# Per-item adapters gathered by GpSimd instead of selected by TensorE, with new chunk counts and a moved style network

## What is computed

```python
hidden = gelu(einsum('bsd,ad->bsa', x, down_W) + down_b)
idx = clip(domain_id, 0, E - 1)
expert_out = einsum('bsa,boa->bso', hidden, expert_W[idx]) + expert_b[idx][:, None, :]
domain_output = where(valid, expert_out, hidden)
hidden = einsum('bsa,da->bsd', domain_output + domain_emb[idx], up_W) + up_b
x = layer_norm(hidden + x) * ln_gamma + ln_beta
...
h = layer_norm(x) * ln_g + ln_b
h_norm = (h - h.mean(1)) * rsqrt(h.var(1) + 1e-08)      # over an item's 64 tokens
sty = relu(hyp(subj_emb[subject_ids]) @ sty_w1 + sty_b1) @ sty_w2 + sty_b2
h = h_norm * softplus(gamma) + beta
gates, idx = top_k(softmax(h @ router_w), 2)
y = sum over the two experts of gate * (relu(h @ w1 + b1) @ w2 + b2)
return x + y
```

## Time and profile before

| | us |
|---|---|
| median of 3 executions | 582.35 (581.31 to 584.63) |
| profiled execution, device time | 582.23 |
| profiled execution, span | 580.3 |
| busy: TensorE, VectorE, ScalarE, GpSimd | 529.5, 379.2, 277.4, 244.4 |
| indirect DMA instructions on GpSimd | 64 scatters (L574), 71 adding stores (L605) |

### The profile page before, as it was taken

One profiled execution on the slowest core, in us unless ns is written; L12 is line 12 of the kernel. 1 busy time (PEld: TensorE's weight loads), 2 busy tenths in 40 slices (PEclk: granted clock), 3 DMA queues, 4 the chain that ended last, 5 costly groups with the idle time before them and its releaser, 6 DMA issues.

```text
span 580.3 us, 15539 instructions
## 1 busy us (share of the span) xinstructions
PE 529.5 (91%) x4386; PEld 445.6 (77%) x4387; DVE 379.2 (65%) x1233; ACT 277.4 (48%) x628; POOL 244.4 (42%) x208
## 2 busy tenths in 40 slices
PE   4977878888776999999999999999999999999993
PEld 3765656566455988988888888888888888888772
DVE  2466989888989868668765464554645655554552
ACT  3547776677563664344253442533424434343432
POOL 2000458888866724766242232322423324223322
PEclk8669797788797999999999999999999999999998
DMA  9465355775454343446644234342342433424222
GB/s 246 152 207 183 110 155 172 254 229 192 165 181 113 83 62 41 102 85 136 133 74 65 38 50 59 40 69 37 46 64 37 62 47 45 55 29 57 39 27 29
DMA packets 78094, 57.58 MB, mean 99 GB/s; under 512 B 51346, under 2 KB 71699, under 8 KB 77907
## 3 DMA queue, kind: packets, MB, share of 16 engines
q1 hardware_dynamic: 63698, 38.37, 25.7%
q0 software_dynamic: 13296, 17.83, 18.0%
q10 hardware_dynamic: 1058, 0.85, 0.7%
HBM read 23.18 MB, written 24.55 MB: 82 GB/s over the span
## 4 chain that ended last, share of the span: by engine, by line
PE 70%; POOL 13%; DVE 6%; issue 4%; DMA 3%; ACT 2%; SPq 1%; POOLq 0%; DVEq 0%; ACTq 0%
PE banks L830 33%; PE banks L846 30%; POOL queues L574 8%; POOL rsT L582 3%; POOL rs L565 2%; PE banks L653 2%; DMA out<-nb,token 1%; DVE w_low L1250 1%; DVE stats L1167 1%; PE banks L713 1%; DMA uw<-up_b 1%; PE banks L693 1%; PE banks L714 1%; DMA rT<-queues 1%; PE banks L727 1%
## 5 line engine op out<-in xcount | busy, mean ns | idle before, releaser
L605 POOL DMA_INDIRECT out<-nb,token x71 | 114.9, 1618 | 221.0 <-ACT nb L1041 196.9
L830 PE MATMUL banks<-rT,w_high 128*128 128x256 f16 (+1 forms) x1248 | 196.7, 265 | 8.4 <-DMA rT<-queues 7.6
L846 PE MATMUL banks<-w_high,stage 128*128 x1136 | 188.1, 273 | 0.9 <-issue 0.2
L830 PE MATMUL banks<-rT,w_low 128*128 128x256 f16 (+1 forms) x624 | 163.3, 264 | 0.0
L846 PE MATMUL banks<-w_low,stage 128*128 x568 | 154.8, 273 | 0.0
L1025 ACT ACTIVATE xb<-banks,feat 128x256 f32<-128x256 f32 (+1 forms) x312 | 120.8, 454 | 52.6 <-PE banks L830 46.3
L830 PEld LDWEIGHTS banks<-rT,w_high 128*128 x1248 | 114.5, 98 | 27.3 <-issue 10.4
L846 PEld LDWEIGHTS banks<-w_high,stage 128*128 128x128 f16 x1136 | 110.4, 98 | 14.8 <-issue 1.9
L1041 ACT ACTIVATE nb<-act,gate 128x256 f32<-128x256 f32 x71 | 32.6, 501 | 179.2 <-DVE act L1508 175.7
L1483 DVE TENSOR_TENSOR stage<-xb,stage 128x512 f16<-128x512 f32 (+1 forms) x156 | 100.6, 645 | 5.3
L1481 DVE CAST stage<-xb 128x512 f16<-128x512 f32 (+1 forms) x156 | 66.6, 427 | 54.3 <-ACT xb L1025 51.6
(11 more groups left out here) (186 smaller groups left out, 516.7 us busy)
## 6 DMA issues: line engine op xcount, KB each, us to landing
stage<-expert_w SPq DMA_DIRECT2D x32, 512.0 KB, 4.6
xb<-x SPq DMA_DIRECT2D x8, 512.0 KB, 6.3
out<-rb SPq DMA_DIRECT2D x8, 512.0 KB, 3.2
queues<-pad_row SPq DMA_DIRECT2D x9, 260.0 KB
out<-nb,token POOLq DMA_INDIRECT x71, 3.9
queues<-h_rows,slot POOLq DMA_INDIRECT x64
b<-exp_b SPq DMA_DIRECT2D x1, 1024.0 KB, 6.5
rT<-queues SPq DMA_TRANSPOSE x39, 4.0
```

What stands on the lines that cost most here:

```text
L605: nc.gpsimd.indirect_dma_start(out=out, out_offset=bass.IndirectOffsetOnAxis(ap=token[:, i.par, s:s + 1], axis=0), in_=yg[:, i.par, s, :], ...
L830: last = nc.tensor.matmul(ps_in(i, c), w[:, at], features(i)[:, v, k, :], start=(n == 0), stop=(n == 3 * DC - 1))
L846: last = nc.tensor.matmul(ps_out(i.par)[:, s, :], v[:, i.par, c, s * P:(s + 1) * P], w[:, at], start=(n == 0), stop=(n == 3 * FC - 1))
```

## The change

GpSimd fetches the adapters itself. VectorE computes row numbers (id x 64 + row), and GpSimd issues 32 indirect loads (`gather`), each of 128 rows of 64 numbers: two items' adapters below each other, 4 loads a group. Those of groups 0 to 3 stand before its loop, those of 4 and 5 at the end of pass 1, those of 6 and 7 at the end of pass 2. TensorE turns them with 4 transposes a group (`turn_rows`), group g+1 in pass g behind up; ScalarE copies them to `wsel` (`copy_adapters`). The table, `select` and its copies are gone. TensorE runs down(0) first, then the item rows, 18 products that nobody reads (`FIRST_WARM`), and group 0's transposes.

Passes have 6, 4, 4, 4, 3, 3, 3, 3 chunks and 2 remain. SyncE loads the next x ahead of the chunks, and a pass's fourth chunk behind the store of x1. The second x waits for group 0's gathers. The ids go out first on ScalarE's queue; the style network's and the norms' constants go out on SyncE's. `style_layer` 2 stands behind down(1), 3 behind the adapters, `style_out` behind up(1); `softplus` stands between `layer_norm` and `scale_features` of group 0 with a table load for Gelu behind it, and `item_gammas` moves to pass 2.

```diff
@@ -54,16 +54,21 @@
-CUTS = [8, 3, 3, 3, 3, 3, 3, 3, 3]
+CUTS = [6, 4, 4, 4, 3, 3, 3, 3, 2]
...
+ROWS_AT = CHUNKS - GROUPS // 2
+ADAPTERS_AT = ROWS_AT - GROUPS
+PAIR = 2 * A
+GATHERS = GROUP // T // 2
...
+FIRST_WARM = 18
@@ -226,9 +233,9 @@
-        table = w_low[0:NONE_ROW + 1, 16 * CHUNK:24 * CHUNK].bitcast(F32)
-        wsel = w_low[0:A, 24 * CHUNK:32 * CHUNK].bitcast(F32)
...
+        wrows = w_low[:, ROWS_AT * CHUNK:CHUNKS * CHUNK].bitcast(F32)
+        wsel = w_low[0:A, ADAPTERS_AT * CHUNK:ROWS_AT * CHUNK].bitcast(F32)
+        table_rows = adapter_w.rearrange("n (o a) -> (n o) a", a=A)
@@ -451,12 +457,15 @@
-                sp.dma_start(ids_i, spread(ids, SUBJECTS)).then_inc(ids_loaded, 16)
-                sp.dma_start(sids_i, spread(subject_ids, SUBJECTS)).then_inc(ids_loaded, 16)
...
+                for dst, src in ((dw[:], down_w), (ab[:, 0:1], down_b)):
+                    sp.dma_start(dst, src).then_inc(down_loaded, 16)
+                for dst, src in ((uw[0:A], up_w), (uw[A:A + 1], up_b)):
...
+                for dst, src in ((g0[:], spread(gamma0, P)), (b0[:], spread(beta0, P)), (hw1, hyp_w1), (feat[:], feature),
+                                 (hw2, hyp_w2), (sw1, sty_w1), (sw2, sty_w2), (rw[:], router_w)):
+                    sp.dma_start(dst, src).then_inc(late_loaded, 16)
+                sp.wait_ge(rows_loaded[0], GATHERS * 16)
@@ -467,12 +476,14 @@
-                    load_weights(i, slice(STAGES if i.g == 0 else 0, None))
-                    if (s2 := back(i, 1)) is not None:
-                        if i.g + 1 < GROUPS:
-                            sp.wait_ge(up_done, s2.g + 1)
-                            load_x(At(s2.half + 1, s2.par))
+                    s2 = back(i, 1)
+                    if s2 is not None and i.g + 1 < GROUPS:
+                        sp.wait_ge(up_done, s2.g + 1)
+                        load_x(At(s2.half + 1, s2.par))
+                    load_weights(i, slice(STAGES if i.g == 0 else 0, 3 if i.g else None))
+                    if s2 is not None:
...
+                        load_weights(i, slice(3, None))
@@ -582,6 +593,17 @@
+                def gather(g):
...
+                    for n in range(g * GATHERS, (g + 1) * GATHERS):
+                        nc.gpsimd.indirect_dma_start(
+                            out=wrows[:, n * A:(n + 1) * A], out_offset=None, in_=table_rows,
+                            in_offset=bass.IndirectOffsetOnAxis(ap=row_no[:, n:n + 1], axis=0)).then_inc(rows_loaded[g], 16)
...
+                pool.wait_ge(rows_known, 2)
+                for g in range(4):
+                    gather(g)
...
                 def body(i):
@@ -594,6 +616,9 @@
+                    if i.g == 1 or i.g == 2:
+                        gather(2 * i.g + 2)
+                        gather(2 * i.g + 3)
@@ -642,22 +667,25 @@
-                def select():
...
-                            last = nc.tensor.matmul(banks[:, 4 + b % 2, k * ITEMS:(k + 1) * ITEMS],
-                                                    table[:, q * 2 * A:(q + 1) * 2 * A], hot_w, start=True, stop=True)
...
+                def turn_rows(g):
...
+                    pe.wait_ge(rows_loaded[g], GATHERS * 16)
+                    wait(pe, adapters_copied, g)
+                    if g == 2:
+                        pe.wait_ge(net_ready, 5)
+                    wait(pe, low_ready, g - 3)
+                    for k in range(GATHERS):
+                        n = g * GATHERS + k
+                        last = nc.tensor.transpose(banks[0:A, 4, k * PAIR:(k + 1) * PAIR], wrows[:, n * A:(n + 1) * A],
+                                                   ident[:])
+                    last.then_inc(rows_turned, 1)
...
                 def style_layer(k):
...
+                    pe.wait_ge(adapters_copied, 2)
@@ -678,27 +706,33 @@
                 def adapter(i):
-                    if isinstance(i.g, int) and i.g == 0:
-                        item_rows()
-                        pe.wait_ge(dom_row, 2)
-                        pe.wait_ge(net_ready, 2)
...
+                    def add_item_rows():
+                        wait_apart(pe, dom_row, (dom_ready, i.g))
+                        wait(pe, place_ready, i.g - 2)
+                        nc.tensor.matmul(ps_dom, item_add[:], bcast(ident[:, bass.ds(i.g * GI, GI)], 2, [P, GI, T]),
+                                         start=True, stop=False)
...
+                    if i.g == 0:
+                        pe.wait_ge(down_loaded, 16 * N_DOWN)
+                    else:
+                        add_item_rows()
...
                     if i.g == 0:
-                        select()
...
+                        item_rows()
+                        for _ in range(FIRST_WARM):
+                            nc.tensor.matmul(banks[:, 2, 0:P], ident[:], ident[:], start=True, stop=True)
+                        turn_rows(0)
+                        pe.wait_ge(dom_row, 2)
+                        pe.wait_ge(net_ready, 2)
+                        add_item_rows()
                     if i.g == 1:
-                        style_layer(3)
...
+                        style_layer(2)
...
+                    pe.wait_ge(adapters_copied, i.g + 1)
@@ -706,13 +740,15 @@
                     if i.g == 1:
-                        style_out()
+                        style_layer(3)
...
+                    if i.g == 1:
+                        style_out()
@@ -730,6 +766,7 @@
                 def back_rows(i):
...
+                    pe.wait_ge(adapters_copied, upto(i.g, 4, GROUPS))
                     if i.g >= FIRST:
@@ -788,9 +825,9 @@
                     if i.g == 1:
...
-                    if i.g == 1:
-                        style_layer(2)
...
+                    if i.g + 1 < GROUPS:
+                        turn_rows(i.g + 1)
@@ -974,23 +1011,35 @@
-                def copy_selected(b):
...
+                def copy_adapters(g):
+                    sc.wait_ge(rows_turned, g + 1)
+                    nc.scalar.activation(wsel[:, g * GI * A:(g + 1) * GI * A], banks[0:A, 4, :],
+                                         ACT.Copy).then_inc(adapters_copied, 1)
...
                 def body(i):
...
                     if i.g == 0:
+                        activate(s1)
+                        cut_high(i, slice(0, 2))
+                        copy_adapters(0)
+                        adapted(s1)
+                        cut_high(i, slice(2, 4))
+                        copy_adapters(1)
+                        cut_high(i, slice(4, None))
+                        return
+                    if i.g == 1:
...
-                        for b in range(SELECTS):
...
+                        cut_high(i, slice(1, 2))
...
-                        cut_high(i, slice(SELECTS + 1, None))
+                        cut_high(i, slice(2, 3))
+                        layer_norm(s2)
+                        softplus()
+                        nc.scalar.preload_act_table(ACT.Gelu)
+                        scale_features(s2)
+                        cut_high(i, slice(3, None))
+                        copy_adapters(2)
@@ -999,6 +1048,8 @@
                     if s3 is not None and s3.g < FIRST:
...
+                    if 1 < i.g < GROUPS - 1:
+                        copy_adapters(i.g + 1)
...
                     if s3 is not None and s3.g < FIRST:
@@ -1007,13 +1058,12 @@
-                iterations(body, after={1: softplus})
+                sc.dma_start(ids_i, spread(ids, P)).then_inc(ids_loaded, 16)
+                sc.dma_start(sids_i, spread(subject_ids, SUBJECTS)).then_inc(ids_loaded, 16)
+                nc.scalar.preload_act_table(ACT.Gelu)
...
+                iterations(body)
@@ -1104,15 +1154,22 @@
+                V.tensor_scalar(part_share[0:A], part_no[0:A], 1.0 / A, None, ALU.mult).then_inc(part_ready, 1)
+                V.tensor_scalar(part_share[upper], part_no[upper], 1.0 / A, -1.0, ALU.mult, ALU.add).then_inc(part_ready, 1)
...
+                link(V.tensor_copy(idf, ids_i))
+                link(V.tensor_scalar(idc, idf, -1.0, float(NONE_ROW), ALU.max, ALU.min))
+                link(V.tensor_scalar(none, idc, 0.0, float(NONE_ROW + 1), ALU.is_lt, ALU.mult))
+                link(V.tensor_tensor(idc, idc, none, ALU.add))
+                dve.wait_ge(part_ready, 2)
+                for half, some in enumerate((slice(0, A), upper)):
+                    of_half = idc[some].rearrange("p (n h) -> p h n", h=2)[:, half]
+                    V.tensor_scalar(row_no[some], of_half, part_share[some, 0:1], float(A), ALU.add,
+                                    ALU.mult).then_inc(rows_known, 1)
@@ -1241,11 +1293,10 @@
                 def cut_low(i, some):
...
+                        if q >= ROWS_AT:
+                            dve.wait_ge(rows_turned, GROUPS)
+                        elif q >= ADAPTERS_AT:
+                            dve.wait_ge(adapt_done, q - ADAPTERS_AT + 1)
@@ -1381,12 +1432,8 @@
                     if i.g == 0:
-                        cut_low(i, slice(0, 1))
```

(7 more changed lines are left out.)

77 lines of the change are left out of this document (19 added, 58 removed).

## The result

The changed kernel took 586.81 us in the median of six runs (585.10 to 588.69), the kernel before 583.93 (581.31 to 585.16) beside it on the same chip: ratio 1.005, 95% interval 1.003 to 1.007. So it is half a per cent slower. I had forecast 582.0, no change; the time lies in the range that I gave, but beyond what I had called no change. The profiled execution took 585.10, its span is 583.1, 2.8 longer than before.

The account below looks back on a forecast made before the run. The end was taken to follow GpSimd's fourth first-moment operation: 31.0 + 20.1 + 22.0 + 22.2 = 95.3 against 96.41, plus a 0.85 wait, less 0.3 us in all. Forecast 582.0 us, range 577.5 to 589.

Parts of the forecast that it names:

- Stage 1: Start to the first marker, GpSimd's first-moment operation for group 0: 31.0 us, 10.5 earlier, gathers replacing the selection.
- Stage 2: First to second marker (first-moment operation of group 1): 20.1 us, 2.1 lost, through ScalarE's longer list.
- Stages 3 and 4: Second to third and third to fourth marker: 22.0 and 22.2 us, 4.6 and 2.7 lost, ScalarE waiting for late fourth chunk.
- The end: After the fourth marker: GpSimd waits once for the item variance, 0.85 us; the end otherwise moves with that marker.
- Standing still for whole cuts: Rival: each VectorE weight cut stops GpSimd's gathers for its full 1.2 us; 590.9 us; chance 0.06.
- Dear gathers: Rival: a gather costs GpSimd 1.83 us with issue; 592.6 us; chance 0.12.
- TensorE at half clock in stage 1: Rival: transposes, item rows, adapters and up before the first marker take 5.5 us more; 587.5 us; chance 0.22.
- The late chunk isn't late: Rival: ScalarE gets the fourth chunk before needing it; 575.5 us, or 579 with slowed gathers; chance 0.18.

Follow-up runs that it names:

- e1: Changed kernel with the fourth chunk's load issued ahead of the store of x1: 579.59 us, ratio 0.990 to the kernel before.
- e8: Changed kernel with warming products on TensorE ahead of the route, 24 in pass 2 and 22 in pass 3: 584.62 us, ratio 0.997.
- e9: Changed kernel with the fourth load ahead of the store and cuts of 6, 3, 4, 4, 3, 3, 3, 3, 3: 608.54 us, ratio 1.006, another chip.
- e4: Kernel before, no gathers, with cuts of 8, 3, 4, 4, 3, 3, 3, 3, 1 and the fourth load behind the store: 594.56 us, ratio 1.014.
- e6: Changed kernel, load still late, with ScalarE's fourth cut at the pass's end and VectorE's low half behind the row fields: 580.15 us, ratio 0.991.
- e3: Changed kernel with warming products on TensorE ahead of the route, 24 in pass 2 and 31 in pass 3: 583.84 us, ratio 0.9995.
- e7: Changed kernel without the 18 warming products in stage 1: 588.79 us, ratio 1.008.

## Why the prediction was wrong

**Stage 1** (forecast 31.0, measured 30.16). Cadence and end of the gathers held: 0.95 + 0.30, and sixteen ended at 29.3. The landing didn't: 2.5 us from the fourth gather's issue instead of 3.9, so that up(0) ended at 22.0 at clock 1.00, not 24.1. TensorE then waited 1.73 us for the second four, whose landing, 6.3 us behind the eighth's issue, I hadn't in the chain. They were turned by 24.35, where I had 24.7; behind that stand the second adapters' copy, two cuts on ScalarE, VectorE's low halves and the moments, as forecast. ScalarE's waits for chunk loads (2.13 and 1.29 us) end before that copy. In e1's chain that ended last the same landing is one piece:

```profile
18.02 6.36 DMA w_low<-adapter_w,row_no
```

Stage 1 was right to 0.8 by compensation, that is by luck.

**Stage 2** (20.1, 20.81). The list of ScalarE with three table loads and then the fourth cut was the chain, as said. VectorE stood still for 4.01 us for that cut:

```profile
40.61 0.31 ACT L942 ACTIVATE w_high<-w_high 128x128 f32<-128x128 f32 x1 [1.18 <-DVE item_beta L1205]
...
47.90 1.23 DVE L1301 SCALAR_TENSOR_TENSOR w_low<-stage,w_high 128x1024 f16<-128x1024 f32 x1 [4.01 <-ACT w_high L951]
```

But ScalarE did have a gap where I had forecast none: layer norm ended at 39.4 and softplus began at 40.61, 1.18 later, since it waited for the style network's last product behind up(1). Up(1) had come late because act(1) stood behind pass 1's first chunk, which landed 6.9 us after its issue at 22.68, and it ran partly at half clock (0.50 at 34 to 36). In other executions of the same code on the first chip this stage took 19.5 to 23.1, and ScalarE's wait for that chunk in them from 1.3 to 2.9 us; in the longest, e8's, the gap ahead of softplus was 3.41. My figure for GpSimd's own list, 19.8 in the expectation of e9, was too long: without the fourth chunk the stage took 18.0 to 18.5 on the other chips.

**Stages 3 and 4: the step that failed** (22.0 and 22.2, measured 23.58 and 25.08). The mechanism is the one forecast, and e1, e4 and e6 show it by undoing it, doing it alone, and moving the cut. The term was mis-sized by 4.5 us, in two ways. First, the landing: 4.5 us in stage 3, where I had 4.7, but 5.8 in stage 4. With the store 0.2 later the cut starts 11.4 behind the marker there instead of 10.0, 1.4 us. My own rows gave 4.4 and 5.7, and I took 4.7, near the quick one, for both. Second, TensorE's route, which has no term in my sum: I added ScalarE's operations up to the logits as if the route were always done in time. At full clock, 1.85 us, it would have ended at 66.5, ahead of layer norm's end at 67.0 (an estimate; e3's logits wait for nothing). It ran at 0.50 in both stages, took 3.58, and ended at 68.2. So the logits came 0.7 later in stage 3, and the way from the best two to the next moments took 4.2 instead of 3.2, because the rows' way back ran at half clock too and ScalarE and VectorE waited 1.60 and 0.89 for it. That is some 1.6 us in each stage by the clock. I forecast that ScalarE would idle for 4 to 6 us and didn't ask what TensorE does in that time. e3, which keeps the clock up and changes nothing else, gives back 2.2 of stage 3.

**The end.** 99.63 + 0.85 against 96.41 is 4.1 late, and so is the marker after it (119.17, before 115.06). SyncE's first row came 3.5 late, but TensorE's expert layers began only 2.4 late (181.13 instead of 178.73), since the first rows landed sooner behind it, and the span is 2.8 longer.

**The rivals.** *Standing still for whole cuts* fell: the four gathers that were slowed most took 1.72 to 2.12 us, 0.8 to 1.2 more, while others beside a cut took 0.95 to 1.24, and sixteen ended at 29.3, not 36.5. The Trainium skill, "SBUF — State Buffer", section "Who interferes with whom", says that a VectorE instruction with two SBUF inputs, as the low half's is, contends with a GpSimd instruction that reads SBUF. The slowed gathers agree with that; why the one at 23.78, inside a cut, took 0.95 isn't shown. *Dear gathers* fell: 0.95, not 1.53. *TensorE at half clock in stage 1* fell for the changed kernel (1.00 from 8 to 32 us). What I read in the earlier trace rows for it, "with TensorE busy throughout", isn't what they say: TensorE was busy for 0.08 of the 2.00 us at 8 to 10. My price of 5.5 was too high by the 1.73 us that TensorE had to spare behind up(0); e7 had the clock down for some 3 us only, which moved up(0) by 2.1 and the first marker by 0.5, so half clock up to the end of up(0) wasn't measured. *The late chunk isn't late* fell, but its price was nearly right: e1, which makes it early, took 579.6, where I had put 579 with slowed gathers (and 575.5 without).

**The chances.** I gave half clock in passes 2 and 3 only a place in the spread of 3 us. As a consequence of the very wait that I forecast it should have been in the sum: 22.0 + 1.6 is stage 3, and 22.2 + 1.6 with the landing's 1.4 makes stage 4 to 0.1.

## What to carry to other kernels

Where a forecast says "this engine waits for x us", go on to the engines that wait for it: here TensorE came out of a gap of 5.5 us at half clock, and work that would have been hidden at 1.85 us was on the path at 3.58. A load that is issued behind a store and consumed on an in-order engine ahead of its urgent work made that engine wait 5.0 and 6.6 us here; issue it ahead of the store (e1) or consume it last (e6), each worth 7 us. Measure on more than one chip: this change is 0.5% slower on one and 2.4% on another, and the mended version 1.0% faster and the same.

## What the runs showed of the hardware

- The granted clock fell from 1.00 to 0.50 within TensorE's idle 5.5 us (60 to 64: 0.63, then 0.50) and stayed there for the 3.58 of route and beyond; with products through the gap it stayed at 1.00 (e3).
- An indirect gather of 128 rows of 64 values costs GpSimd 0.95 us and 0.30 of issue, as much as a scatter of 128 rows four times as long (0.96); beside VectorE's cuts some take 1.72 to 2.12 and others 0.95 to 1.24.
- A gather's way from issue to landing was 2.5 us in a stretch with a DMA share of 0.07 (12 to 14 us), and 6.3 us beside x and chunk loads with a share of 1.06 (18 to 22 us).
- A load of 512 KB issued behind a store of 512 KB landed 4.5 and 5.8 us after its issue.
- On chips where the kernel before takes 595 to 601 us, ScalarE was idle for 9 to 19 us in stage 1 of each of nine profiled executions with gathers, mostly with nothing on the core that the profile could name, and in none of the eight with gathers among the ten earlier profiles. The kernel before has such stops there too, later and shorter (four of them, 5.0 us at most).
